# A two-layer attention kernel on one core: the weighted sums of eight steps go one at a time instead of in pairs

## What is computed

```python
qkv = layernorm(x) @ w_qkv + b_qkv
attn = softmax(einsum('bqhd,bkhd->bhqk', q, k) * scale)
x = x + einsum('bhqk,bkhd->bqhd', attn, v) @ w_out + b_out
```

## Time and profile before

| | before |
|---|---|
| median of three runs | 869.61 us |
| the profiled execution | 874.13 us |
| its span | 872.4 us |
| PE busy | 803.8 us, 92% |
| ACT busy | 604.4 us, 69% |
| DVE busy | 518.5 us, 59% |
| POOL busy | 163.8 us, 19% |
| TensorE clock granted, mean | 0.956 of full |

### The profile page before, as it was taken

The page is one execution under the profiler, slowest core; times in us unless marked ns, Lnnn a source line. Parts: engine busy times, 40 slices in busy tenths (PEclk is TensorE's granted clock), DMA queues, the critical chain, the costliest instruction groups (busy, mean ns, idle before and its releaser), DMA issues.

```text
span 872.4 us, 14477 instructions
## 1 busy us (share of the span) xinstructions
PE 803.8 (92%) x5139; PEld 382.3 (44%) x5139; DVE 518.5 (59%) x1518; ACT 604.4 (69%) x683; POOL 163.8 (19%) x198
## 2 busy tenths in 40 slices
PE   7885987999999999999999999999999989899988
PEld 6221332335443445335543545345434445246665
DVE  6304344477757675678567675678357762466564
ACT  4594776767887788767886688768886876673112
POOL 2702103410322112410341030320311011000100
PEclk9797998999999999999999999999999999899979
DMA  3541333322514332522433241532242241301300
GB/s 75 99 79 41 61 62 67 80 43 44 98 36 96 59 55 56 119 46 41 89 81 59 44 81 40 112 62 44 43 107 46 45 69 26 82 7 31 74 1 25
DMA packets 45309, 52.91 MB, mean 61 GB/s; under 512 B 15920, under 2 KB 33968, under 8 KB 45232
## 3 DMA queue, kind: packets, MB, share of 16 engines
q1 hardware_dynamic: 45232, 51.92, 30.7%
HBM read 5.45 MB, written 4.19 MB: 11 GB/s over the span
## 4 chain that ended last, share of the span: by engine, by line
PE 60%; ACT 13%; DVE 9%; issue 5%; ACTq 0%; DVEq 0%
PE O L621 21%; PE S L606 14%; ACT Pr L840 9%; PE BC L635 5%; PE BC L627 3%; PE BC L732 3%; PE BC L718 2%; PE A L559 2%; PE BC L672 2%; PE S L824 2%; PE BC L654 2%; DVE rsel L1151 1%; DVE rgt L1150 1%; ACT hT L880 1%; ACT L840 1%
## 5 line engine op out<-in xcount | busy, mean ns | idle before, releaser
L840 ACT ACTIVATE Pr<-S 128x1024 f32<-128x1024 f32 x512 | 491.7, 1029 | 157.1 <-PE S L606 153.8
L621 PE MATMUL O<-Pr,Va 128*32 128x512 f32 x2048 | 272.8, 642 | 9.8 <-DVE OT L1059 9.1
L606 PE MATMUL S<-Qs,Ks 49*128 49x512 f32 x1024 | 218.4, 474 | 28.9 <-ACT Pr L840 25.4
L606 PEld LDWEIGHTS S<-Qs,Ks 49*128 49x128 f32 x1024 | 88.5, 188 | 181.3 <-ACT Pr L840 129.6
L621 PEld LDWEIGHTS O<-Pr,Va 128*32 128x32 f32 x2048 | 52.1, 112 | 122.4 <-issue 112.0
L488 POOL TENSOR_TENSOR q1l<-q1T,q1h 128x1024 fp32r<-128x1024 f32 x8 | 19.1, 2386 | 228.1 <-DVE q1h L1109 228.1
L1133 DVE TENSOR_REDUCE r<-BC 128x1 f32<-128x512 f32 x64 | 41.2, 685 | 30.7 <-PE BC L672 30.7
L451 POOL TENSOR_SCALAR xn<-X,ln 128x128 f32<-128x128 f32 x56 | 46.0, 833 | 33.3 <-DVE ln L972 33.3
L1059 DVE STREAM_TRANSPOSE OT<-O 128x512 f32<-128x512 f32 x32 | 22.8, 714 | 42.0 <-PE O L621 41.8
L855 ACT ACTIVATE tT<-BC,cols 128x512 f32<-128x512 f32 x32 | 23.4, 777 | 31.1 <-PE BC L627 31.1
L502 POOL TENSOR_TENSOR tokx<-tokx_new,tok_bias 128x1024 f32<-128x1024 f32 x8 | 18.9, 2365 | 120.9 <-DVE tokx_new L978 120.9
(11 more groups left out here) (187 smaller groups left out, 988.4 us busy)
## 6 DMA issues: line engine op xcount, KB each, us to landing
Qs<-qh SPq DMA_DIRECT2D x128, 64.0 KB, 2.3
Ks<-kh SPq DMA_DIRECT2D x128, 64.0 KB, 2.3
Q1s<-q1h SPq DMA_DIRECT2D x64, 128.0 KB, 2.4
X<-in_x_dram SPq DMA_DIRECT2D x8, 512.0 KB, 4.1
Qs<-ql SPq DMA_DIRECT2D x64, 64.0 KB, 2.4
Ks<-kl SPq DMA_DIRECT2D x64, 64.0 KB, 2.3
attnT<-On SPq DMA_DIRECT2D x128, 32.0 KB, 2.0
Q1s<-q1l SPq DMA_DIRECT2D x32, 128.0 KB, 2.4
```

Of the source, the lines that this page charges most:

```text
L606: mm = pe.matmul(S[:, c, a * HALF:(a + 1) * HALF], Ks[head, j, kb * P:(kb + 1) * P], Qs[head, j, c * HALF:(c + 1) * HALF], start=True, sto ...
L621: mm = pe.matmul(O[r:r + 32, :], Va[:, kb, 2 * j + a, :], Pr[:, (STEPS * n + s) % 3, c, a * HALF:(a + 1) * HALF], start=(kb == 0), stop=(k ...
L840: act.activation(Pr[:, g % 3, c, :], S[:, c, :], ACT.Exp, scale=SCALE).then_inc(probs_ready, 1)
```

## The change

`one_by_one(n)` goes, and `sums_behind(n, s)` says which weighted sums stand behind the scores of step s: in images 0 and 7, and now in the steps 17 to 24 (THIN) of every image, the one of s-1; in the other steps as before.

```diff
+THIN = range(17, 25)
-def one_by_one(n):
-    return n in (0, IMAGES - 1)
+def sums_behind(n, s):
+    if n in (0, IMAGES - 1) or s in THIN:
+        return (s - 1,) if s > 0 else ()
+    return (s - 2, s - 1) if s % 2 == 0 and s > 0 else ()
...
                     scores(n, s, 0)
                     scores(n, s, 1)
-                    if s > 0 and (s % 2 == 0 or one_by_one(n)):
-                        if not one_by_one(n):
-                            weighted(n, s - 2)
-                        weighted(n, s - 1)
+                    for behind in sums_behind(n, s):
+                        weighted(n, behind)
...
-                if not one_by_one(n):
-                    weighted(n, STEPS - 2)
-                weighted(n, STEPS - 1)
+                for behind in sums_behind(n, STEPS):
+                    weighted(n, behind)
```

## The result

The changed kernel takes 892.11 us (890.55 to 894.46), the kernel before 868.76: a ratio of 1.0249, with a 95% interval of 1.0212 to 1.0286. It is slower, as forecast, but by some 21 to 23 us where 14 were forecast, and the median lies outside the range.

A forecast was written before the change was run, and what follows sets the result against it. PE, busy 92% of the span, was taken to bound the kernel, with two chains through steps 17 to 25. Order +15.4 us and clock -1.4 gave +14.0: median 869.6 to 883.6 us, range 874 to 890.

The forecast's parts named there:

- two chains: Step 21's k matmul to the turn of r, 4.24 us; step 23's k matmul to hot, 7.62 us; both lengths unchanged.
- The order's size: Steps 18 to 23: step 23's L559 comes 2.57 us later an image, 15.4 us over six images.
- waits for DVE: PE waits 0.53 us at step 20's L672 and 1.05 us before L678, for DVE's reductions.
- splits: Steps 17 to 24: four pairs become eight singles, each split costing 0.15 us, 0.6 us an image.
- the turned O: Step 17: the sum of 16 must wait until DVE has turned O, 0.41 us, set against a removed exponential wait.
- the sum of 22: It now stands ahead of step 23's L559, adding 1.00 us, and leaves the time where PE waited for hot anyway.
- The clock: Behind PE's wait for hot, step 26: six falls stay, some may begin inside the longer wait; -1.4 us in all.
- The price of a fall before: Step 26 of the kernel before: the pair takes 3.55 us instead of 1.85, so 1.70 us lost an image.
- DVE does not bind: Steps 20 and 22: DVE has idle time, PE alone counts; 1.44 us an image, 878.2 us; chance 0.15.
- The clock stays up: Behind L686 no fall in all six images: 15.4 - 10.2, +5.2 us, 874.8 us; chance 0.11.
- Faster: Delay an image under 1.70 us with the loss behind L686 gone: 8.6 - 10.2 = -1.6 us, 868.0 us; chance 0.04.
- More falls: The waits before L678 and before L686 each bring a clock fall: +25.6 us, 895.2 us; chance 0.08.

The follow-up runs named there:

- thin_21_22: Kernel before with singles only at steps 21 and 22, so the sum of 20 goes ahead of step 21's k matmul: 881.5 us, ratio 1.0114.
- before_squares_late: Kernel before, with POOL's squares of q and k waiting from image 1 on until hot is made: 851.2 us, ratio 0.9745.
- the filled pair: Dummy matmuls before PE's wait for hot, eight in the changed kernel, six in the kernel before: 882.7 and 864.1 us; 96.14 and 93.51 us an image.
- before_filled: Kernel before with six dummy matmuls ahead of PE's wait for hot in images 1 to 6: 864.1 us, ratio 0.9928.
- thin_23_24: Kernel before with singles only at steps 23 and 24, so only the sum of 22 goes ahead of step 23's k matmul: 879.5 us, ratio 1.0104.
- thin_17_22: Changed kernel with singles at steps 17 to 22 only, sums 22 and 23 again a pair at 24: 878.1 us, ratio 1.0110.

## Why the prediction was right and wrong

- **Direction and the order's mechanism: right.** An extra sum ahead of the L559s, two chains that start from it, both as long as before (4.24 and 7.62 us). thin_21_22 isolates the first, before_squares_late the second.
- **The order's size: right.** 2.57 us an image forecast; 2.55 from the first L675 to the last L562 (14.44 - 11.89), and 2.63 of whole image with the clock out of both kernels. So near a hit is in part luck, since waits at the first L672 and L675 differ by 0.1 to 0.2 us an image from run to run. Its parts are shown too: 1.20 of waits for DVE (forecast 0.53 + 1.05, less the 0.45 of waits for exponentials that they cover), and 0.80 for splits, exponentials and the turned O. The other 0.63 is only there while PE waits for hot: it is the sum of 22, which left that wait.
- **The clock: wrong, and the step that failed.** The prediction said of the falls: "A fall may begin inside the longer wait, where a low clock costs nothing", and took -1.4 us. The fall did begin inside the wait, in each of the images 1 to 6, but it did not bring an unchanged low stretch forward. The clock stayed low from 388.84 to 395.66, 6.82 us, where it had been low for 3.41. The forecast's -1.4 us came out at +6.1 by steps 26 and 27 (6 x 1.01), or +5.4 by the filled pair (6 x 0.90). With it the sum is 15.4 + 5.4 to 6.1, 20.8 to 21.5 us, where six times 3.53 is 21.2 and the ratio's 2.49% of 869 is 21.6.
- **The price of a fall before** was right: 1.70 us in the working, 1.67 by steps 26 and 27 of before and before_filled.
- **The rivals.** "DVE does not bind" fell: both waits are there, released by L1133's and L1138's results. "The clock stays up" fell. "Faster" fell with them. "More falls" had the right sign and nearly the right sum, but not the mechanism: there is still one fall an image, only longer, and none behind the wait of 1.00 us before L681.
- **The range** took the clock's term from a falling price to none, and had no case in which one fall becomes longer. The rows held nothing that excluded it, and nothing that foretold it either.

## What to carry to other kernels

Before moving work on a busy engine, find the instructions from which chains on other engines start, and put nothing ahead of them: work that fills a wait behind such an instruction is free, the same work ahead of it costs its whole length. A wait of the matmul engine of 1.6 to 2.2 us mostly had a second price in the clock here, 1.7 us where the fall came after the wait and 2.7 where it came within it, and four dummy matmuls of 1 us in all took most of it away. When such a wait is near, leave room in the range for a fall that costs more than the one in the rows. Then ask what makes the wait: here it was GpSimd's squares beside small VectorE operations, and moving them gave more than any order of the sums.

## What the runs showed of the hardware that was not expected

- One fall of the clock costs more when it comes before PE's wait ends: step 26 took 5.34 us, against 4.41 when the fall came after the wait (thin_23_24), and 2.81 without one, all with the same instructions.
- Waits of equal length do not bring the same falls: with 1.65 us thin_17_22 had none in two of six images and a fall within the wait in two, and with 1.63 us the kernel before had one after the wait in each of the six.
- Two GpSimd operations of 1.9 us stretched two VectorE operations of 0.25 and 0.27 us to 1.52 and 1.96 us.
